# Fused patch embedding, attention and mixture-of-experts layer: the gate bias moves into the router's product, and its logits are read from PSUM

## The chip, the core and the metric

One core of a Trainium2 chip runs the whole program. The metric is the device time of one execution in microseconds (us); lower is better. Engines are named as in the profile: PE is TensorE (PEld its weight loads), DVE is VectorE, ACT is ScalarE, POOL is GpSimd, SP is the queue that issues DMAs.

## The reference

```
h   = patches(x) @ W.T + b + pos_emb                  # 64 images, 121 patches of 192
h   = concat([h, txt])                                # 249 tokens per image
h   = h + quantised_attention(layernorm(h))           # 12 heads, integer softmax
x2  = layernorm(h)
s   = softmax(x2 @ gate_w + gate_b)                   # the router: 16 experts
s_b = s + bias
    # best 4 of 8 pairs of experts by s_b, then the best 4 experts in them
w   = s of the chosen experts * 2.5                   # else 0
y   = sum_e w_e * (silu(x2 @ Wu_e + bu_e) * (x2 @ Wg_e + bg_e)) @ Wd_e + w @ bd + shared expert
out = h + y
```

What matters here is the line of `s`: a product of 192 by 16 per token, plus a bias of 16, and a softmax over the 16 values, for which their maximum is subtracted first.

## The kernel before

The kernel works image by image, 64 in all, as a software pipeline over five images at once. A list `ORDER` (L304 to L355) names every stage with a shift and a number, for instance `("turn", -1, 0)`: in step j this is stage "turn", number 0, of image j-1. Every engine walks through the same list and issues those stages that it has code for, in that order. There are no other priorities: each engine's queue is strictly in the list's order, and semaphores join the engines. Setup (weights rounded, scaled by LIFT = 256, transposed) comes first; on VectorE it is a chain in which each instruction waits for the one before (`link`, L685), and the other engines wait for the chain's count `VSETUP`.

The tokens of an image lie in two blocks of up to 128 partitions. The normalised rows x2 are kept as float16 (the rounded value twice, then the rounding rest) with three columns of ones behind them. They are transposed through PSUM to `x2T`, five blocks of 128 rows. The router's product ("route", L1155 to L1161) is ten matmuls of 16 columns, five blocks for each token block, against the weights `GW`; the fifth block's weights are the last 64 rows of the weight in rows 0 to 63 and zeros in rows 64 to 127, where rows 64 to 66 meet the ones. The expert products use the same three rows of ones for their biases, from `UGB`.

The PSUM bank `pX` (2 KB per partition) is shared by many products: patch embedding, the turns (transposes) of both normalised inputs, q/k, v, the transposed probabilities, the projection, the router, the chosen weights. PE keeps its order by `take_x(signal, value)` (L1056): before it writes pX it waits for the signal that its last user handed in, which tells that this content was read; and it hands in its own. The PSUM banks `pS` (scores and the exponent's polynomial), `pU` (expert products), `pW`, `pY`, `pO` have other users.

Around the router, `ORDER` (L334 to L336) has in this sequence, with the engine in brackets:

- route, image j-3 (PE), writes pX
- split, image j-1 (POOL): float16 parts of the first normalised input, read by turn
- act, pair 2 of image j-4 (DVE, L1028)
- logit, image j-3 (DVE, L1003): logits = pX / LIFT + bias, to SBUF
- lmax, image j-3 (DVE, L1008): maximum over the 16 values, of the SBUF logits
- expo, unit 2 of image j-2 (DVE, L962): four instructions, each with an accumulator read
- u, unit 3 of image j-2 (PE, L1120 and L1121): four matmuls to pS
- turn, number 0 of image j-1 (PE, L1082): three transposes to pX
- power, unit 3 of image j-2 (DVE, L953)
- mmG, pair 3 of image j-4 (PE, L1183): ten matmuls to pU
- below, unit 4 of image j-2 (ACT, L607)
- copy, number 0 of image j-1 (ACT, L650): reads the turn from pX
- below_max, image j-3 (DVE, L1012): difference of logits and maximum, to `lx`
- then square, unit 3 (ACT), quot, unit 4 (DVE, L948), gate, pair 3 of image j-4 (DVE, L1023, which needs mmG of pair 3), turn, number 1 (PE)

The gates stage (ACT, L662 and L663) then takes two Silu of the difference, from which the softmax's exponentials are made. The v product (PE, L1102 and L1104) is read from pX on DVE by L937. The shared down bias (L1192) is a product with the transposed chosen weights, which ACT copies (L668).

Of the kernel before, what the change touches and what calls it, by code (L numbers as in the profile page):

```python
# [14 lines left out]
ALU = mybir.AluOpType  # L15
# [6 lines left out]
F16 = mybir.dt.float16  # L22
# [20 lines left out]
def fused_layer(nc, x, txt, tok_W, tok_b, pos_emb, w_qkv, b_qkv, w_proj, b_proj, sw_qkv, sw_proj,  # L43
# [34 lines left out]
    with ctx:  # L78
        def sb(name, shape, dt=F32):
            return ctx.enter_context(nc.sbuf_tensor(name, shape, dt))  # L80
# [48 lines left out]
        def cut(words):  # L129
# [57 lines left out]
        pr8 = sb("pr8", [P, 2, D], I8)  # L187
        x2 = sb("x2", [P, 2, D])
        x2s = sb("x2s", [P, 2, BLOCKS * P], F16)
        logit = sb("logit", [P, 2, E])  # L190
        lmax = sb("lmax", [P, 2])
        lx = sb("lx", [P, 2, E])
        sil = sb("sil", [P, 2, 2, E])
# [25 lines left out]
        pY = ps("pY", [P, 512])  # L219
        pXb, pXh, pXi = (pX[:, :].bitcast(t) for t in (BF16, F16, I16))  # L220
        pXt = pX[:, :].rearrange("p (t c) -> p t c", t=2)[:, :, 0:D]
        pYt = pY[:, :].rearrange("p (t c) -> p t c", t=2)[:, :, 0:D]


# [19 lines left out]
            sem(n) for n in ("vr_done", "lo_done", "gr_done", "pr_done", "prT_ps"))  # L244
        prT_done, pv_done, o_q, ob_done, pj_ps, pq_done = (
            sem(n) for n in ("prT_done", "pv_done", "o_q", "ob_done", "pj_ps", "pq_done"))
        h2_done, g_ps, lg_done, rt_done, lx_done, sil_done = (
            sem(n) for n in ("h2_done", "g_ps", "lg_done", "rt_done", "lx_done", "sil_done"))
        w3_done, w3_ps, w3T_done, up_ps, gp_ps, wb_ps = (
            sem(n) for n in ("w3_done", "w3_ps", "w3T_done", "up_ps", "gp_ps", "wb_ps"))  # L250
        up_done, gate_done, act_done, dn_done, y_done = (
# [6 lines left out]
        def cc(n, rows=P):  # L258
            return cst[0:rows, n:n + 1]

        V_TOK, V_QKV, VSETUP = 4, 85, 102
        RT = 22


# [25 lines left out]
        for t in range(2):  # L290
# [41 lines left out]
            ("store", -5, -1), ("act", -4, 1), ("turn2", -3, 1), ("quot", -2, 3), ("copy2", -3, 1),  # L332
            ("pick", -4, 2), ("down", -4, 1), ("gate", -4, 2), ("silu", -4, 3), ("low", -2, 0),
            ("norm", -1, -1), ("low", -2, 1), ("top", -2, 5), ("route", -3, -1), ("split", -1, -1),  # L334
            ("act", -4, 2), ("logit", -3, -1), ("lmax", -3, -1), ("expo", -2, 2), ("u", -2, 3), ("turn", -1, 0),
            ("power", -2, 3), ("mmG", -4, 3), ("below", -2, 4), ("copy", -1, 0), ("below_max", -3, -1),  # L336
            ("peak", -2, 5), ("square", -2, 3), ("sum", -2, 2), ("quot", -2, 4), ("gate", -4, 3),
            ("turn", -1, 1), ("alpha", -2, 2), ("grow", -2, 0), ("expo", -2, 3), ("copy", -1, 1),
# [208 lines left out]
        def _(act):  # L547
# [43 lines left out]
            for j in STEPS:  # L591
                for stage, i, k in stages(j):
# [17 lines left out]
                    elif stage == "square":  # L610
                        n, b = NTOK[k % 2], k % 2
                        act.wait_ge(u_ps, UNITS * i + k + 1)
                        after(act, y_made, UNITS * i + k - 1)
                        sc_.activation(sq[b][0:n, :].rearrange("p (b c) -> p b c", b=2),  # L614
                                       pS[0:n, :, 0:2 * TOKENS], ACT.Square,
                                       bias=cc(C_HL, n)).then_inc(sq_done, 1)
                    elif stage == "share":
                        n, b = NTOK[k % 2], k % 2
                        act.wait_ge(al_done, UNITS * i + k + 1)
                        after(act, gr_done, UNITS * i + k - 1)  # L620
                        for m in range(PER):
                            c = slice(m * TOKENS, (m + 1) * TOKENS)
                            a = sc_.activation(v[b][0:n, c], y[b][0:n, c], ACT.Copy,  # L623
                                               scale=alpha[b][0:n, m:m + 1])
                        a.then_inc(vr_done, 1)
                    elif stage == "copyp":
                        n, b = NTOK[k % 2], k % 2
                        act.wait_ge(prT_ps, UNITS * i + k + 1)
                        after(act, pv_done, UNITS * i + k - 1)
                        pt = pXi.rearrange("p (m b q) -> p m b q", m=PER, b=2)  # L630
                        for t in range(2):
                            sc_.activation(probT[b][0:NTOK[t], :, t, 0:n].bitcast(I16),  # L632
                                           pt[0:NTOK[t], :, t, 0:n], ACT.Relu,
                                           bias=cc(C_OB, NTOK[t])).then_inc(prT_done, 1)
                    elif stage == "outq":
                        act.wait_ge(pv_done, UNITS * i + 2 * k + 2)
                        after(act, ob_done, GROUPS * (i - 1) + k + 1)
                        sc_.activation(o8[:, k, :], pO[:, 0:TOKENS], ACT.Copy,
                                       scale=cc(C_O)).then_inc(o_q, 1)
                    elif stage == "qkq":  # L640
                        act.wait_ge(qk_ps, QK * i + k + 1)
                        after(act, cv_done, GROUPS * (i - 1) + k % GROUPS + 1)
                        sc_.activation(qk8[:, k, :], pX[:, 0:TOKENS], ACT.Identity,  # L643
                                       bias=qk_bias[:, k:k + 1],
                                       scale=qk_scale[:, k:k + 1]).then_inc(qk_q, 1)
                    elif stage == "copy":
                        act.wait_ge(xt_ps[0], 2 * i + k + 1)
                        after(act, v_ps, i)
                        after(act, qk_ps, QK * i)
                        sc_.activation(xT[:, :, k * P:(k + 1) * P],  # L650
                                       pXh[:, 0:3 * P].rearrange("p (b c) -> p b c", b=3),
                                       ACT.Copy).then_inc(xt_done[0], 1)
                    elif stage == "copy2":
                        act.wait_ge(xt_ps[1], 2 * i + k + 1)
                        after(act, gp_ps, PAIRS * (i - 1))
                        after(act, g_ps, i - 1)
                        sc_.activation(x2T[i % 2][:, :, k * P:(k + 1) * P],
                                       pXh[:, 0:BLOCKS * P].rearrange("p (b c) -> p b c", b=BLOCKS),
                                       ACT.Copy).then_inc(xt_done[1], 1)
                    elif stage == "gates":  # L660
                        act.wait_ge(lx_done, i + 1)
                        sc_.activation(sil[:, 0], lx[:], ACT.Silu, bias=cc(C_DOWN)).then_inc(sil_done, 1)  # L662
                        sc_.activation(sil[:, 1], lx[:], ACT.Silu, bias=cc(C_UP),  # L663
                                       scale=-1.0).then_inc(sil_done, 1)
                    elif stage == "copyw":
                        act.wait_ge(w3_ps, i + 1)
                        after(act, wb_ps, (PAIRS - 1) * i)
                        sc_.activation(w3T[:], pXb[0:SPLIT * QUAD, 0:COLS], ACT.Copy).then_inc(w3T_done, 1)  # L668
                    elif stage == "silu":
                        n = EVEN if k == 0 else 2 * EVEN  # L670
                        act.wait_ge(up_ps, PAIRS * i + k + 1)
                        if k == 2:
                            act.wait_ge(dn_done, PAIRS * i + 1)
                        else:
                            after(act, gate_done, PAIRS * i + {0: 0, 1: -1}.get(k, k - 1))
                        sc_.activation(up[k % 2][:, 0:n], pU[:, 0, 0:n], ACT.Silu,  # L676
                                       scale=1.0 / LIFT).then_inc(up_done, 1)
# [3 lines left out]
        def _(dve):  # L681
# [125 lines left out]
            for b, p0, signal, n in ((1, REST, ld_f1, 10), (2, 0, ld_f2, 5)):  # L807
# [5 lines left out]
                for dst, src in ((UG[p0:P, b], ug_rows[b][p0:P]), (GW[p0:P, b, :], gw_rows[p0:P, b, :])):  # L813
                    if len(dst.shape) == 4:
                        dst, src = (a.rearrange("p e m h -> p (e m h)") for a in (dst, src))
                    link(stt(out=dst, in0=src, scalar=LIFT, in1=dst, op0=ALU.mult, op1=ALU.subtract))
            assert chain[0] == VSETUP, chain[0]

            dve.wait_ge(s_asetup, PSETUP)
# [84 lines left out]
            for j in STEPS:  # L904
                for stage, i, k in stages(j):
# [89 lines left out]
                    elif stage == "residual":  # L995
# [1 line left out]
                        after(dve, y_done, i - 1)  # L997
                        stt(out=h2[i % 2][:], in0=pr8[:], scalar=cc(C_S3), in1=h[i % 2][:], op0=ALU.mult,
                            op1=ALU.add).then_inc(h2_done, 1)
                    elif stage == "logit":  # L1000
                        dve.wait_ge(g_ps, i + 1)
                        after(dve, lx_done, i)
                        stt(out=logit[:].rearrange("p t e -> p (t e)"), in0=pX[:, 0:2 * E],  # L1003
                            scalar=1.0 / LIFT, in1=gb2[:].rearrange("p t e -> p (t e)"),
                            op0=ALU.mult, op1=ALU.add).then_inc(lg_done, 1)
                    elif stage == "lmax":
                        dve.wait_ge(lg_done, i + 1)
                        ve.tensor_reduce(lmax[:], logit[:], AX, ALU.max).then_inc(rt_done, 1)  # L1008
                    elif stage == "below_max":
                        dve.wait_ge(rt_done, RT * i + 1)  # L1010
                        after(dve, sil_done, 2 * i)
                        tt(lx[:], logit[:], lmax[:].unsqueeze(2).broadcast_to([P, 2, E]),  # L1012
                           ALU.subtract).then_inc(lx_done, 1)
                    elif stage == "gate":
                        m = EVEN if k == 0 else 2 * EVEN
# [22 lines left out]
        def _(pe):  # L1038
# [29 lines left out]
            for j in STEPS:  # L1068
                for stage, i, k in stages(j):
# [84 lines left out]
                        a.then_inc(pj_ps, 1)  # L1154
                    elif stage == "route":  # L1155
                        pe.wait_ge(xt_done[1], 2 * (i + 1))
                        take_x(lg_done, i + 1)
                        for t in range(2):
                            for m in range(BLOCKS):
                                a = mm(pX[:, t * E:(t + 1) * E], x2T[i % 2][:, m, t * P:(t + 1) * P],  # L1160
# [83 lines left out]
```

## Time and profile before

| | us |
|---|---|
| median of 3 runs (3519.58 to 3520.66) | 3520.66 |
| the profiled execution's own time | 3518.62 |
| its span, first to last instruction | 3516.8 |

| engine | busy us | share |
|---|---|---|
| PE | 3381.6 | 96% |
| DVE | 3368.5 | 96% |
| ACT | 3153.6 | 90% |
| POOL | 806.2 | 23% |

The profile is one execution; its time is 2.04 us below the median of the runs shown. Busy time is the union of an engine's instructions. Matmuls overlap each other in the array, so a matmul's duration (270 ns for 250 columns) is longer than the distance to the next one's start; pace is read from the starts.

### The profile page before, as it was taken

Reading aid. Unit: us, or ns where it says so; the run is one execution under the profiler, and the core shown is the slowest. Engines: PE = TensorE matmul, PEld = TensorE weight load, DVE = VectorE, ACT = ScalarE, POOL = GpSimd, SP = SyncE. Lnnn points to the kernel's source line nnn. Section 1 sums busy time; section 2 is a strip of 40 time slices with the busy share of each in tenths; the row PEclk is TensorE's granted clock in tenths of the full one; section 3 lists DMA queues with packets and bytes.
Section 4 is the critical chain, followed back from the end, with each engine's and each line's share of the span. In section 5 each row is a group of like instructions: output and inputs, shape, how many; then the busy total and the mean of one; then the engine's idle time right before and its main releaser. Section 6 shows DMA issues by size and latency. Waiting matters only on the chain.

```text
span 3516.8 us, 98077 instructions
## 1 busy us (share of the span) xinstructions
PE 3381.6 (96%) x30764; PEld 2898.6 (82%) x30764; DVE 3368.5 (96%) x10279; ACT 3153.6 (90%) x6228; POOL 806.2 (23%) x1647
## 2 busy tenths in 40 slices
PE   1589999999999999999999999999999999999999
PEld 1368888888888888888888888888888888888888
DVE  6699999999999999999999999999999999999995
ACT  2799999999999999999999999999999999999992
POOL 3222222222222222222221221222222222222210
PEclk9789999999999999999999999999999999999999
DMA  5101001000000000000000110100000000000000
GB/s 125 27 14 25 25 16 26 25 20 23 25 20 23 24 22 21 24 23 20 25 24 18 25 25 16 26 25 17 25 25 20 23 25 21 22 24 23 20 10 8
DMA packets 157123, 85.77 MB, mean 24 GB/s; under 512 B 51451, under 2 KB 154370, under 8 KB 156610
## 3 DMA queue, kind: packets, MB, share of 16 engines
q1 hardware_dynamic: 153692, 78.82, 9.0%
q8 instruction: 253, 4.15, 0.5%
q14 instruction: 260, 2.13, 0.2%
q10 hardware_dynamic: 2918, 0.67, 0.1%
HBM read 54.89 MB, written 12.24 MB: 19 GB/s over the span
## 4 chain that ended last, share of the span: by engine, by line
PE 92%; DVE 1%; issue 1%; ACT 0%; POOLq 0%; DVEq 0%; POOL 0%
PE pU L1183 33%; PE pY L1209 20%; PE pX L1075 5%; PE pX L1132 5%; PE pS L1120 4%; PE pS L1111 4%; PE pS L1121 4%; PE pX L1094 3%; PE pW L1195 3%; PE pO L1142 2%; PE pY L1192 1%; PE pX L1102 1%; PE pX L1088 1%; PE pX L1151 1%; PE pX L1082 1%
## 5 line engine op out<-in xcount | busy, mean ns | idle before, releaser
L1183 PE MATMUL pU<-x2T,UG 128*128 128x250 f16 x8704 | 1231.6, 270 | 1.0 <-ACT work L676 0.9
L1183 PEld LDWEIGHTS pU<-x2T,UG 128*128 128x128 f16 x8704 | 823.0, 97 | 108.7 <-ACT work L676 1.5
L1209 PE MATMUL pY<-WD,work 128*128 128x192 f32 (+1 forms) x4352 | 810.0, 328 | 0.0
L1209 PEld LDWEIGHTS pY<-WD,work 128*128 128x128 f32 (+1 forms) x4352 | 690.8, 187 | 3.9
L962 DVE SCALAR_TENSOR_TENSOR work<-work,cst 128x249 f32<-128x249 f32 (+1 forms) x1536 | 658.6, 484 | 8.4 <-issue 4.3
L623 ACT ACTIVATE work<-work,alpha 128x249 f32<-128x249 f32 (+1 forms) x1536 | 648.3, 509 | 15.2 <-DVE alpha L974 14.0
L607 ACT ACTIVATE work<-a,room 128x249 bf16<-128x249 int8 (+1 forms) x1536 | 648.3, 514 | 0.0
L1183 PE MATMUL pU<-x2T,UGB 67*128 67x250 f16 x2176 | 592.4, 272 | 0.0
L942 DVE TENSOR_REDUCE rmax<-a 128x4 f32<-128x996 int8 (+1 forms) x384 | 452.9, 1179 | 40.9 <-ACT a L598 40.9
L632 ACT ACTIVATE passing<-pX,cst 128x512 int16<-128x512 int16 (+3 forms) x768 | 480.8, 687 | 6.9 <-PE pX L1132 3.5
L598 ACT ACTIVATE a<-pS,cst 128x996 int8<-128x996 f32 (+1 forms) x384 | 421.4, 1097 | 70.3 <-PE pS L1111 70.1
L614 ACT ACTIVATE work<-pS,cst 128x996 f32<-128x996 f32 (+1 forms) x384 | 419.5, 1092 | 56.8 <-PE pS L1121 56.8
L983 DVE SCALAR_TENSOR_TENSOR work<-work 128x996 bf16<-128x996 bf16 (+1 forms) x384 | 453.1, 1180 | 0.1
L497 POOL TENSOR_SCALAR qb<-qk 128x249 bf16<-128x249 int8 x192 | 103.6, 540 | 1308.6 <-ACT qk L643 1307.5
L676 ACT ACTIVATE work<-pU 128x500 f32<-128x500 f32 (+1 forms) x576 | 326.0, 566 | 72.6 <-PE pU L1183 72.6
L1023 DVE TENSOR_TENSOR work<-pU,work 128x500 f32<-128x500 f32 x512 | 342.0, 668 | 17.3 <-PE pU L1183 17.1
L1028 DVE TENSOR_TENSOR work<-work,pW 128x500 f32<-128x500 f32 x512 | 339.2, 662 | 13.3 <-PE pW L1195 12.6
L1120 PE MATMUL pS<-work,ident 128*128 128x498 bf16 (+1 forms) x768 | 293.3, 382 | 7.7 <-ACT a L598 2.8
L1121 PE MATMUL pS<-work,identx 128*128 128x498 bf16 (+1 forms) x768 | 290.5, 378 | 0.0
L1111 PE MATMUL pS<-kb,qz 128*128 128x249 bf16 (+1 forms) x1536 | 232.6, 275 | 29.1 <-DMA qz<-qb 21.0
L979 DVE TENSOR_SCALAR work<-work 128x996 int16<-128x996 int16 (+1 forms) x384 | 255.2, 665 | 0.8 <-ACT work L623 0.7
L643 ACT ACTIVATE qk<-pX,qk_bias,qk_scale 128x249 int8<-128x249 f32 x384 | 219.1, 570 | 39.6 <-PE pX L1094 39.5
(209 smaller groups left out, 5337.5 us busy)
## 6 DMA issues: line engine op xcount, KB each, us to landing
img<-in_x_dram SPq DMA_DIRECT2D x896, 23.5 KB
img<-in_x_dram SPq DMA_DIRECT2D x768, 21.4 KB
qz<-qb SPq DMA_DIRECT2D x768, 15.6 KB, 1.8
h<-in_txt_dram SPq DMA_DIRECT2D x64, 96.0 KB, 2.0
out_dram<-yout SPq DMA_DIRECT2D x64, 96.0 KB
out_dram<-yout SPq DMA_DIRECT2D x64, 90.8 KB
WD<-in_L_ffn_Wd_dram SPq DMA_DIRECT2D x1, 1536.0 KB, 7.6
work<-in_L_ffn_Wu_dram SPq DMA_DIRECT2D x2, 512.0 KB, 6.6
```

Of the source, the lines that this page charges most:

```text
L598: sc_.activation(a8[b][0:n, :].rearrange("p (b c) -> p b c", b=2), pS[0:n, :, 0:2 * TOKENS], ACT.Copy, scale=cc(C_S, n)).then_inc(a_done, 1)
L607: a = sc_.activation(g16[b][0:n, c], a8[b][0:n, c], ACT.Relu, bias=room[b][0:n, m:m + 1])
L614: sc_.activation(sq[b][0:n, :].rearrange("p (b c) -> p b c", b=2), pS[0:n, :, 0:2 * TOKENS], ACT.Square, bias=cc(C_HL, n)).then_inc(sq_don ...
L623: a = sc_.activation(v[b][0:n, c], y[b][0:n, c], ACT.Copy, scale=alpha[b][0:n, m:m + 1])
L632: sc_.activation(probT[b][0:NTOK[t], :, t, 0:n].bitcast(I16), pt[0:NTOK[t], :, t, 0:n], ACT.Relu, bias=cc(C_OB, NTOK[t])).then_inc(prT_don ...
L942: ve.tensor_reduce(rmax[b][0:n, :], a8[b][0:n, :].rearrange("p (m c) -> p m c", m=PER), AX, ALU.max).then_inc(mx_done, 1)
L962: a = stt(out=y[b][0:n, c], in0=sq[b][0:n, c], scalar=cc(C_KC, n), in1=pw[b][0:n, c].bitcast(BF16), op0=ALU.add, op1=ALU.mult, accum_out=r ...
L983: stt(out=grown[b][0:n, :], in0=p16[b][0:n, :].bitcast(BF16), scalar=6.0, in1=v[b][0:n, :], op0=ALU.subtract, op1=ALU.mult).then_inc(gr_do ...
L1120: mm(pS[0:n, m, 0:2 * TOKENS], ident[0:n, 0:n], g16[b][0:n, c], start=True, stop=False)
L1121: a = mm(pS[0:n, m, 0:2 * TOKENS], identx[0:n, 0:n], q16[b][0:n, c], start=False, stop=True)
L1183: a = mm(pU[:, s, q * EVEN:(q + 1) * EVEN], weights, x2T[i % 2][0:w, m, 0:EVEN], start=m == 0, stop=m == BLOCKS - 1)
L1209: a = mm(pY[0:n, t * 256:t * 256 + D], (act_[k % 2] if k else up[0])[:, c:c + n], WD[:, e, :], start=k == 0 and t == 0, stop=e == E - 1, s ...
```

## The change

The bias is put into the router's product: it is scaled by LIFT, split into three float16 parts, and the parts are written into rows 64, 65 and 66 of the fifth weight block, where the ones are. The product in PSUM is then LIFT times the complete logits. The logit stage is dropped from `ORDER`; maximum and difference read the lifted values from PSUM, and the gates divide by LIFT in their scale. The bank pX after the router is handed on by the signal of the difference (`lx_done`) in place of that of the logit (`lg_done`). `gb2` is still loaded. Nothing else in `ORDER` moves.

```diff
-        logit = sb("logit", [P, 2, E])
+        gb_parts = sb("gb_parts", [P, SPLIT, E], F16)
...
+        lifted = pX[:, 0:2 * E].rearrange("p (t e) -> p t e", t=2)
...
-        V_TOK, V_QKV, VSETUP = 4, 85, 102
+        V_TOK, V_QKV, VSETUP = 4, 85, 111
...
-            ("act", -4, 2), ("logit", -3, -1), ("lmax", -3, -1), ("expo", -2, 2), ("u", -2, 3), ("turn", -1, 0),
+            ("act", -4, 2), ("lmax", -3, -1), ("expo", -2, 2), ("u", -2, 3), ("turn", -1, 0),
...
-                        sc_.activation(sil[:, 0], lx[:], ACT.Silu, bias=cc(C_DOWN)).then_inc(sil_done, 1)
+                        sc_.activation(sil[:, 0], lx[:], ACT.Silu, bias=cc(C_DOWN),
+                                       scale=1.0 / LIFT).then_inc(sil_done, 1)
                         sc_.activation(sil[:, 1], lx[:], ACT.Silu, bias=cc(C_UP),
-                                       scale=-1.0).then_inc(sil_done, 1)
+                                       scale=-1.0 / LIFT).then_inc(sil_done, 1)
...
+            ones3 = slice(REST, ONES)
+            whole = gb2[ones3, 0, :]
+            link(ts(whole, whole, LIFT, None, ALU.mult))
+            for s in range(SPLIT):
+                if s:
+                    link(tt(whole, whole, gb_parts[ones3, s - 1], ALU.subtract))
+                link(ve.tensor_copy(gb_parts[ones3, s], whole))
+            link(ts(GW[ones3, 3, :], gb_parts[ones3, 0], identf[ones3, REST:REST + 1], None, ALU.mult))
+            for s in range(1, SPLIT):
+                link(stt(out=GW[ones3, 3, :], in0=gb_parts[ones3, s], scalar=identf[ones3, REST + s:REST + s + 1],
+                         in1=GW[ones3, 3, :], op0=ALU.mult, op1=ALU.add))
...
-                    elif stage == "logit":
+                    elif stage == "lmax":
                         dve.wait_ge(g_ps, i + 1)
                         after(dve, lx_done, i)
-                        stt(out=logit[:].rearrange("p t e -> p (t e)"), in0=pX[:, 0:2 * E],
-                            scalar=1.0 / LIFT, in1=gb2[:].rearrange("p t e -> p (t e)"),
-                            op0=ALU.mult, op1=ALU.add).then_inc(lg_done, 1)
-                    elif stage == "lmax":
-                        dve.wait_ge(lg_done, i + 1)
-                        ve.tensor_reduce(lmax[:], logit[:], AX, ALU.max).then_inc(rt_done, 1)
+                        ve.tensor_reduce(lmax[:], lifted, AX, ALU.max).then_inc(rt_done, 1)
                     elif stage == "below_max":
                         dve.wait_ge(rt_done, RT * i + 1)
                         after(dve, sil_done, 2 * i)
-                        tt(lx[:], logit[:], lmax[:].unsqueeze(2).broadcast_to([P, 2, E]),
+                        tt(lx[:], lifted, lmax[:].unsqueeze(2).broadcast_to([P, 2, E]),
                            ALU.subtract).then_inc(lx_done, 1)
...
                     elif stage == "route":
                         pe.wait_ge(xt_done[1], 2 * (i + 1))
-                        take_x(lg_done, i + 1)
+                        take_x(lx_done, i + 1)
```

## Rows read from the trace of the kernel before

**Rows 1.** The page, busy time by engine: us, share of the span, instructions.
```profile
PE 3381.6 (96%) x30764; PEld 2898.6 (82%) x30764; DVE 3368.5 (96%) x10279; ACT 3153.6 (90%) x6228; POOL 806.2 (23%) x1647
PE 92%; DVE 1%; issue 1%; ACT 0%; POOLq 0%; DVEq 0%; POOL 0%
```

**Rows 2.** Busy table by stretch, steady part; then granted clock, DMA share and GB/s.
```profile
600.00:1600.00 1000.00, 998.55 (x9192) 862.52 (x9190) 989.02 (x3047) 934.79 (x1858) 232.70 (x479) 1.00 0.09 22
...
2006.40:2058.60 52.20, 52.16 (x483) 45.11 (x481) 51.65 (x160) 48.90 (x98) 12.17 (x25) 1.00 0.09 23
```

**Rows 3.** Timeline of PE around one router (start, us, operation); last, weight loads of turn.
```profile
2003.63 0.40 PE L1160 MATMUL pX<-GW,x2T 128*128 128x16 f16 x10
...
2004.76 0.33 PE L1082 MATMUL pX<-ident,xs 128*128 128x128 f16 x3
2004.93 0.59 PE L1183 MATMUL pU<-x2T,UG 128*128 128x250 f16 x4
...
2005.46 0.59 PE L1183 MATMUL pU<-x2T,UG 128*128 128x250 f16 x4
2005.89 0.27 PE L1183 MATMUL pU<-x2T,UGB 67*128 67x250 f16 x1
...
L1082 PEld LDWEIGHTS pX<-ident,xs 128*128 128x128 f16 x384 | 32.2, 99 | 25.9 <-POOL xs L534 9.5 <-issue 4.6
```

**Rows 4.** Timeline of DVE over the same stretch.
```profile
2004.31 0.18 DVE L1003 SCALAR_TENSOR_TENSOR logit<-pX,gb 128x32 f32<-128x32 f32 x1
2004.53 0.19 DVE L1008 TENSOR_REDUCE lmax<-logit 128x2 f32<-128x32 f32 x1
2004.71 0.48 DVE L962 SCALAR_TENSOR_TENSOR work<-work,cst 128x249 f32<-128x249 f32 x1
...
2006.32 0.41 DVE L953 TENSOR_SCALAR work<-work 121x996 int16<-121x996 int16 x1
2006.65 0.18 DVE L1012 TENSOR_TENSOR lx<-logit,lmax 128x32 f32<-128x32 f32 x1
...
2007.27 0.67 DVE L1023 TENSOR_TENSOR work<-pU,work 128x500 f32<-128x500 f32 x1
```

**Rows 5.** Instructions on the logit tile: ns least/median/most, first and last start.
```profile
L1003 DVE SCALAR_TENSOR_TENSOR logit<-pX,gb x64: 173/179/192, 174.4 to 3458.3; 128x32 f32<-128x32 f32 x64
...
L1012 DVE TENSOR_TENSOR lx<-logit,lmax x64: 181/183/191, 176.7 to 3458.8; 128x32 f32<-128x32 f32 x64
```

**Rows 6.** Waits of 600 to 3000 us; then the timeline at one v product.
```profile
DVE v L937 <- PE pX L1104: 13.9, 44, 0.4
...
1829.70 0.25 PE L1104 MATMUL pX<-v_add,ones 128*128 128x192 bf16 x1
...
1829.99 0.56 DVE L937 TENSOR_TENSOR v<-pX,v_scale 128x384 int8<-128x384 f32 x1 [0.32 <-PE pX L1104]
```

**Rows 7.** Timeline of the start-up.
```profile
52.47 32.54 SPq L378 DMA_DIRECT2D UGB<-b_parts  x51
...
62.24 0.17 DVE L816 SCALAR_TENSOR_TENSOR GW<-gw_rows,GW 128x16 f16<-128x16 f32 x1
62.46 0.35 DVE L910 TENSOR_TENSOR h<-pX,pos 121x192 f32<-121x192 f32 x1
...
98.21 1.02 PE L1111 MATMUL pS<-kb,qz 128*128 128x249 bf16 x4 [21.04 <-DMA qz<-qb]
```

**Rows 8.** Timeline of PE at one shared down bias.
```profile
1788.44 0.66 PE L1192 MATMUL pY<-BD,w3T 96*128 96x192 bf16 x6 [0.30 <-ACT w3T L668]
```

**Rows 9.** Start-up: timeline of PE, then the busy table with the granted clock.
```profile
110.93 0.39 PE L1120 MATMUL pS<-work,ident 121*121 121x498 bf16 x1 [1.27 <-ACT work L614]
...
166.09 0.61 PE L1111 MATMUL pS<-kb,qz 128*121 128x249 bf16 x4 [1.27 <-ACT a L598]
...
167.10:170.50 3.40, 1.38 (x4) 0.59 (x5) 3.32 (x8) 3.40 (x8) 3.00 (x6) 0.50 0.25 58
...
132.90:136.30 3.40, 2.76 (x12) 1.85 (x13) 3.23 (x11) 2.43 (x7) 1.94 (x3) 0.51 0.02 5
```

More of the change, by code:

```diff
@@ L246, in fused_layer @@
             sem(n) for n in ("prT_done", "pv_done", "o_q", "ob_done", "pj_ps", "pq_done"))
-        h2_done, g_ps, lg_done, rt_done, lx_done, sil_done = (
-            sem(n) for n in ("h2_done", "g_ps", "lg_done", "rt_done", "lx_done", "sil_done"))
+        h2_done, g_ps, rt_done, lx_done, sil_done = (
+            sem(n) for n in ("h2_done", "g_ps", "rt_done", "lx_done", "sil_done"))
         w3_done, w3_ps, w3T_done, up_ps, gp_ps, wb_ps = (
```

## The prediction

> **What bounds the kernel now.** I read the page's engine line first: TensorE is busy 96% of the span and VectorE 96% [rows 1], so neither the matmuls nor the vector work can be dismissed. The busy table by stretch then takes the start-up out of the average: in a thousand microseconds of the steady part PE is busy 998.55 and VectorE 989.02, and in one image's period of 52.20 us PE is busy 52.16 and VectorE 51.65 [rows 2]. The reader is to see that PE has 0.04 us of visible idle per image and VectorE 0.55. The chain of waits puts nearly everything on PE, and the timeline agrees: five matmuls of 250 columns start within 0.53 us (2004.93 to 2005.46, [rows 3]), about 0.106 us each, with no step between stages. PE is the bound, VectorE is just behind it. The wait table of the steady part has only one regular wait of VectorE for PE, at the v product: 13.9 us in 44 images, 0.3 us each [rows 6]. A saved VectorE instruction therefore buys nothing by itself; a wait put into PE's queue costs its full length.
>
> **The operation removed.** The logit instruction takes 179 ns, 64 times [rows 5], and the next dependent one starts 0.22 us after it [rows 4]. That is 0.22 us per image, 14 us in all, taken from VectorE, which is not the bound. Its gain is only that maximum, four exponent instructions, power and difference come 0.22 us earlier.
>
> **Maximum and difference read PSUM.** No row shows these two on PSUM. The nearest is the logit instruction itself: reading 32 elements from PSUM took 179 ns, the difference of 32 elements from SBUF 183 ns [rows 5]. So I take 0, with 0 and +0.05 us per image as ends. The Trainium skill (VectorE: DVE Perf Modes, the section on the TRN2 errata) gives VectorE instructions with a PSUM source a fixed 120 cycles against 58 at 0.96 GHz: an estimate of 0.065 us more for each of the two, which speaks against this change. By that rule the sum would be 61 x 0.13 = 8 us longer; the 179 against 183 ns does not bear it out.
>
> **Bias in the product, scale in the gates.** The router still issues ten matmuls; the three rows of the last weight block were zero and are streamed already. The two gate activations get another immediate scale. Both cost nothing, without needing cover.
>
> **Setup.** Nine small chained VectorE instructions are added (three casts, two subtractions, one scaling, three combinations). The nearest takes 0.17 us and the following one starts 0.22 us after it [rows 7], so 9 x 0.2 = 1.8 us, before the first normalisation. It is covered: the SP queue issues the late bias rows from 52.47 us for 32.54 us, and PE stands idle 21.04 us until 98.21 for the first query DMA, issued behind them [rows 7]. I cost it at nothing; without that cover, 1.8 us once.
>
> **The order of the shared PSUM bank.** This is the step that decides. PE may overwrite pX after the router's product only when its reader is done. The reader was the logit instruction; now it is the difference. Between router and next user (the first turn of image i+2) PE has only the u product: router at 2003.63, turn at 2004.76 [rows 3]. Before, logit ran from 2004.31 to 2004.49, so turn found the bank free [rows 3, 4]. In VectorE's order, between maximum and difference, stand four exponent instructions (2004.71 to 2006.32, a pitch of 0.40 us) and power (0.33 us to the next start): the difference starts at 2006.65 [rows 4]. Nothing in the change moves it forward except the 0.22 us of logit. So:
> - the difference starts at 2006.65 - 0.22 = 2006.43 and ends at 2006.61;
> - an inter-engine hand-over took 0.04 us at the v product (the last matmul ends at 1829.95, v starts at 1829.99) [rows 6], and the turn's weight load takes 0.10 us [rows 3]: turn's matmul at 2006.75;
> - it ran at 2004.76, so PE stands 1.99, say 2.00 us per image, of which some 1.8 are visible as idle.
>
> Behind the waiting turn in PE's queue stand mmG of pair 3, the second turn, mmU of pair 4 and the q/k products. ScalarE's copy waits for the turn, and square behind it. VectorE waits at the gate of pair 3: its matmuls visibly end at 2006.16 [rows 3] and would end 2.00 later, 2008.16, while VectorE would be there at 2007.27 - 0.22 = 2007.05 [rows 4]. So VectorE, too, loses 1.1 us at once.
>
> **Can the delay be made up within the image?** VectorE runs 1.1 - 0.22 = 0.9 us late against PE's 2.0, but where it already waits for PE, at v, it takes on PE's whole lateness [rows 6]. From there to the next router both carry the same 2.0, and the next difference comes 2.0 late again. PE's one larger gap, 0.30 us at the shared down bias, waits for ScalarE's copy [rows 8], behind work that VectorE releases, so it stays. I recover nothing; the bound is that 0.30 us, and 0.24 us if VectorE reached maximum right when the product lands (2003.63 + 0.40 + 0.04 = 2004.07 instead of 2004.31 [rows 3, 4]). That leaves 1.46 us as the low end per image, 2.1 as the high one.
>
> **Sum.** 62 images have a router product followed by a turn; the first lies in the start-up, where PE idles anyway. 61 x 2.00 = 122 us. The profiled execution took 3518.62 us (span 3516.8), so 3640.6. The median of the runs shown is 3520.66, 2.04 above it: **3643 us**.
>
> **Rivals.**
> *Shorter stall.* Part of PE's lateness is recovered as above, or VectorE leads. 1.46 to 1.9 us in 61 images is 89 to 116 us: 3610 to 3637; a little more hidden slack would make it 3600. For it: latencies hide small gaps in PE's row. Against: PE's pitch never relaxes. Chance 0.20.
> *The stall also lowers the clock.* The granted clock is 1.0 throughout the steady part [rows 2], where PE never stands for long. In the start-up PE stood 1.27 us before 110.93 and the next matmul still took 0.39 us; it stood 1.27 us before 166.09 too, and the stretch from 167.10 shows 0.50 [rows 9], the lower level, 1.2 GHz. A new idle of 1.8 us in each image lies above both. The shortest slow stretch there, 132.90 to 136.30 at 0.51 [rows 9], did 3.4 us x 0.5 = 1.7 us less work. If a third of the images pay it, 20 x 1.7 = 34 us more: 3677; if all, 3747. Against: around the new gap PE works densely, in the start-up it doesn't. Chance 0.22.
> *Faster: VectorE is the true bound.* If PE's busy row hid 2.0 us of slack per image between turn and v, PE would catch up before v, and the 0.22 us x 64 = 14 us of the logit stage would show: 3507. It decides from 2.0 us of hidden slack on. Against: the 0.106 us pitch and the 0.04 us of idle; and the 1.1 us new wait at the gate of pair 3 falls on VectorE itself. Chance 0.03.
> *The new wait does not bind*, because turn waits for something as late anyway: no change, 3520. Against: turn started at full pitch after u [rows 3]. Chance 0.02.
> The remaining 0.03 is for a stall that grows beyond 2.1 us per image, by ScalarE falling behind too: 3650 and above.
>
> **How the numbers follow.** The forecast has 0.50. The range 3608 to 3702 takes in it, most of the shorter stall and the clock case up to 35 falls (3643 + 59); about 0.2 is left outside. 0.2% of the time, 7 us, is about what a measurement of this kernel can tell from no change. Faster by more 0.03, within 0.02, slower by more 0.95.
>
> **What would show it.** Right: a PE idle of some 1.8 us before turn (L1082's place) released by the difference, in some 61 images; a new VectorE wait of about 1.1 us at the gate multiplication; the period from difference to difference 54.2 instead of 52.2 us; maximum and difference at 180 to 190 ns; the first score matmul still near 98 us. Wrong: a period of 52 us; a turn released by anything else; maximum or difference near 250 ns; a granted clock below 1.0 in the steady part (the clock rival); a gate that doesn't wait (then VectorE leads).

## The result and the profile after

The changed kernel takes 3660.22 us (median of 3, 3658.25 to 3662.45) against 3520.66 before: ratio 1.0399, 95% interval 1.0384 to 1.0413. That is 139.6 us more, where 122 were forecast, inside the range.

The page first, engine line and chain, to be held against [rows 1]:

```profile
PE 3414.9 (93%) x30764; PEld 2908.9 (80%) x30764; DVE 3380.3 (92%) x10224; ACT 3162.7 (86%) x6228; POOL 778.6 (21%) x1647
PE 3%; DVE 1%; issue 0%; ACT 0%; POOLq 0%; POOL 0%; DVEq 0%
```

TensorE has fallen from 96% to 93% and VectorE from 96% to 92%. The chain, 92% on PE before, now accounts for 4% of the span: it can't be followed through, so it names nothing. The wait table of the whole run does (who waited, for whom: total, times, longest):

```profile
PE pX L1090 <- DVE lx L1020: 108.1, 62, 2.0
```

L1090 is the turn, L1020 the difference: 62 waits, one per image with a router followed by a turn, 1.74 us each. There was no such row before. The timeline of PE around one router, answering to [rows 3], and of VectorE, to [rows 4]:

```profile
2139.48 0.40 PE L1168 MATMUL pX<-GW,x2T 128*128 128x16 f16 x10
2140.39 0.37 PE L1129 MATMUL pS<-work,identx 121*121 121x498 bf16 x1
2142.51 0.33 PE L1090 MATMUL pX<-ident,xs 128*128 128x128 f16 x3 [1.74 <-DVE lx L1020]
2143.64 0.27 PE L1191 MATMUL pU<-x2T,UGB 67*128 67x250 f16 x1
```

```profile
2140.15 0.18 DVE L1016 TENSOR_REDUCE lmax<-pX 128x2 f32<-128x32 f32 x1
2140.25 0.47 DVE L975 SCALAR_TENSOR_TENSOR work<-work,cst 128x249 f32<-128x249 f32 x1
...
2141.85 0.42 DVE L966 TENSOR_SCALAR work<-work 121x996 int16<-121x996 int16 x1
2142.18 0.19 DVE L1020 TENSOR_TENSOR lx<-pX,lmax 128x32 f32<-128x32 f32 x1
...
2144.01 0.68 DVE L1031 TENSOR_TENSOR work<-pU,work 128x500 f32<-128x500 f32 x1 [1.13 <-issue]
```

The last of the u matmuls starts at 2140.39 and would be followed at a pitch of 0.21, at 2140.60; the turn starts at 2142.51. The stall is 1.91 us. The turn starts 0.14 us after the difference ends (2142.18 + 0.19). VectorE pays in its turn: 1.13 us idle at the gate of pair 3. The row names no releaser ("issue"), but the pair's matmuls end visibly at 2143.64 + 0.27 = 2143.91, and the gate starts at 2144.01.

The bank read by maximum and difference costs nothing, as against [rows 5] (ns least/median/most, first and last start):

```profile
L1016 DVE TENSOR_REDUCE lmax<-pX x64: 175/182/192, 176.3 to 3600.0; 128x2 f32<-128x32 f32 x64
L1020 DVE TENSOR_TENSOR lx<-pX,lmax x64: 174/182/191, 178.4 to 3600.2; 128x32 f32<-128x32 f32 x64
```

and the maximum before, from SBUF:

```profile
L1008 DVE TENSOR_REDUCE lmax<-logit x64: 185/186/189, 174.6 to 3458.6; 128x2 f32<-128x32 f32 x64
```

The difference took 183 ns from SBUF and takes 182 from PSUM; the maximum took 186 and takes 182.

There is a second loss. The busy table from one difference to the next, three images in a row, then two stretches of the middle one, answering to [rows 2] and [rows 9] (the third number from the end is the granted clock):

```profile
1978.38:2032.40 54.02, 52.25 (x480) 44.98 (x480) 51.76 (x160) 48.94 (x97) 11.69 (x25) 1.00 0.09 22
2032.40:2088.15 55.75, 53.95 (x480) 45.95 (x480) 51.85 (x159) 49.17 (x97) 11.60 (x25) 0.97 0.08 21
2088.15:2142.18 54.03, 52.25 (x480) 44.97 (x480) 51.78 (x160) 48.94 (x97) 11.69 (x25) 1.00 0.09 22
...
2033.00:2037.00 4.00, 4.00 (x27) 3.15 (x26) 1.71 (x4) 2.83 (x6) 0.00 (x0) 0.61 0.02 4
2037.00:2041.00 4.00, 4.00 (x35) 3.28 (x33) 4.00 (x13) 3.73 (x11) 0.00 (x0) 1.00 0.00 0
```

A period without a fall of the clock is mostly 54.03 to 54.13 us (52.12 to 52.22 before); in either kernel a few are 0.2 to 0.5 us longer. In the middle one the clock is at the lower of its two levels, 1.2 GHz, for most of the stretch right behind the gap: 27 matmuls in 4 us where the next 4 us hold 35, and the period is 1.65 us longer. Counted from the starts of all 64 differences, 14 of the 58 periods of the steady part are long in this way, 44 are not. The trace has just 14 stretches of low clock there, and each begins within 0.5 us behind a turn that had waited. The kernel before has none. Such counts are those of one profiled execution of each kernel; the times of the others, 1 to 7 us apart, leave room for a few falls more or less. So the 139.6 us are 61 x 1.92 = 117 for the wait, plus 14 x 1.65 = 23 for the clock, 140 in all.

### The profile page after: what moved, and what is told of

Its sections match the earlier page's. It is cut to its first block and busy times, and to the rows that moved or that the text cites. A ratio compares the mean times of both kernels' runs of the same rounds, so it can differ in the third digit from the quotient of the medians.

```text
span 3658.4 us, 98022 instructions
## 1 busy us (share of the span) xinstructions
PE 3414.9 (93%) x30764; PEld 2908.9 (80%) x30764; DVE 3380.3 (92%) x10224; ACT 3162.7 (86%) x6228; POOL 778.6 (21%) x1647
## 5 line engine op out<-in xcount | busy, mean ns | idle before, releaser
L1191 PE MATMUL pU<-x2T,UG 128*128 128x250 f16 x8704 | 1251.5, 272 | 1.1 <-ACT work L678 0.9
L1191 PEld LDWEIGHTS pU<-x2T,UG 128*128 128x128 f16 x8704 | 832.0, 98 | 115.6 <-ACT work L678 1.5
L498 POOL TENSOR_SCALAR qb<-qk 128x249 bf16<-128x249 int8 x192 | 78.5, 409 | 1473.0 <-ACT qk L644 1473.0
```

The lines of the kernel that those rows point to most:

```text
L1191: a = mm(pU[:, s, q * EVEN:(q + 1) * EVEN], weights, x2T[i % 2][0:w, m, 0:EVEN], start=m == 0, stop=m == BLOCKS - 1)
```

## The experiments

Ratios are to the kernel before, run on the same chip. The theory: the time is lost because the bank pX is handed on by the difference, and the loss is the way of VectorE to the difference less what PE has to do meanwhile. The rivals: reading PSUM, the bias rows or the setup cost it; VectorE is the bound; the idle itself, by way of the clock, is the larger part.

### The difference moved ahead of the exponents

```diff
-  ("act", -4, 2), ("lmax", -3, -1), ("expo", -2, 2), ("u", -2, 3), ("turn", -1, 0),
+  ("act", -4, 2), ("lmax", -3, -1), ("below_max", -3, -1), ("expo", -2, 2), ("u", -2, 3), ("turn", -1, 0),
-  ("copy", -1, 0), ("below_max", -3, -1),
+  ("copy", -1, 0),
```

> The changed kernel with one stage moved: the difference directly behind the maximum, ahead of the four exponent instructions and power. Hand-over theory: the difference ends 0.4 us after the maximum starts, and the u product on PE covers that, so the stall of turn goes altogether: 3520 us within 5, PE idle before turn below 0.1 us per image, granted clock 1.0 in the steady part. Rival 1 (the cost lies in reading PSUM, in the bias rows or in the setup): nothing of it depends on the order, 3650 to 3660. Rival 2 (VectorE is the true bound, and the missing logit shows once the wait is gone): 3507 to 3512.

3527.15 us, ratio 1.0019 (1.0010 to 1.0028). All but 7 of the 139.6 us come back with one entry of a list moved, everything else of the change in place: rival 1 falls. The hand-over theory expected 3520 within 5 and no stall left, so it missed by 2 us. The 7 are some 0.11 us in each period (mostly 52.24 to 52.33). Their place, in the timelines of VectorE and PE:

```profile
2009.93 0.19 DVE L1020 TENSOR_TENSOR lx<-pX,lmax 128x32 f32<-128x32 f32 x1
...
2009.94 0.37 PE L1129 MATMUL pS<-work,identx 121*121 121x498 bf16 x1
2010.26 0.33 PE L1090 MATMUL pX<-ident,xs 128*128 128x128 f16 x3
```

PE would be free at 2009.94 + 0.21 = 2010.15, the difference ends at 2010.12, the turn starts 0.14 later, at 2010.26. No row calls this an idle: the last u matmul, lasting 0.37, covers it. The same wait is left at 0.11 us.

### The rest of the wait covered

```diff
-  ("expo", -2, 2), ("u", -2, 3), ("turn", -1, 0),
+  ("expo", -2, 2), ("u", -2, 3), ("pick", -4, 3), ("turn", -1, 0),
-  ("pick", -4, 3), ("below", -2, 5), ("silu", -4, 4),
+  ("below", -2, 5), ("silu", -4, 4),
```

> As the first experiment (difference directly behind the maximum), and the product that spreads the weights of pair 3 (two matmuls, 0.21 us on PE) moved from behind mmG of pair 4 to just ahead of turn. Theory: the 0.11 us per image by which that kernel was slower than the one before is the rest of the same hand-over (difference ends at 2010.12, turn starts at 2010.26, PE free at 2010.15); 0.21 us of work in between covers it: 3520 within 3, ratio 1.000, period 52.17. Rival (the 0.11 us are a cost of reading PSUM or of VectorE's order): stays at 3527.

3520.67 us against 3519.33, ratio 1.0004 (0.9995 to 1.0013); periods mostly 52.12 to 52.23 again. The theory holds to 0.1 us per image. It is also the verdict on the idea itself: with no wait left, dropping 64 VectorE instructions gains nothing that can be measured. Rival 2 of the first experiment (3507) falls with it. VectorE waits the saved time away at v: 0.4 us per image in the stretch from 600 to 3000 us, where [rows 6] have 0.3.

```profile
DVE v L950 <- PE pX L1112: 19.2, 46, 0.5
```

### The wait shortened, lengthened, and put in alone

Difference between exponents and power:

```diff
-  ("turn", -1, 0), ("power", -2, 3),
+  ("turn", -1, 0), ("below_max", -3, -1), ("power", -2, 3),
...
-  ("copy", -1, 0), ("below_max", -3, -1),
+  ("copy", -1, 0),
```

> The changed kernel with the difference between the exponent instructions and power, so 0.33 us earlier than in the change and 1.6 us later than directly behind the maximum. Hand-over theory: the stall follows the place of the difference one to one: 1.90 - 0.33 = 1.57 us per image, 61 x 1.57 = 96 us, 3616 without falls of the clock; with a third to all of the falls of the changed kernel (15 x 1.65 us) 3616 to 3640. Rival (a fixed cost of any late hand-over): same as the change, 3660.

Difference behind the next quotient:

```diff
-  ("below_max", -3, -1), ("peak", -2, 5), ("square", -2, 3), ("sum", -2, 2), ("quot", -2, 4),
+  ("peak", -2, 5), ("square", -2, 3), ("sum", -2, 2), ("quot", -2, 4), ("below_max", -3, -1),
```

> The changed kernel with the difference 0.5 us later still, behind the next quotient (and the sum). Hand-over theory: stall 1.90 + 0.52 = 2.42 us per image, 61 x 2.42 = 148 us, 3668 without falls of the clock. Clock theory: an idle of 2.2 us visible per image lowers the clock more often than one of 1.75 us (15 images in the change): 20 to 40 images x 1.65 us, 3700 to 3735. If the falls depend on where the gap lies against a fixed beat rather than on its length, their number may also drop to none: 3668.

And the kernel before with a single line changed:

```diff
-                        take_x(lg_done, i + 1)
+                        take_x(lx_done, i + 1)
```

> The kernel before with one line of the change: the router hands its bank on by the signal of the difference; the logit stage, the bias addition and the SBUF reads stay. Hand-over theory: the whole loss and a little more, since logit stands ahead of the maximum again: the difference at 2006.65 instead of 0.32 earlier, a stall of 2.2 us per image, 61 x 2.2 = 134 us, 3655 without falls of the clock, up to 3690 with them. Rival 1 (PSUM reads or bias rows cost the time): 3520 to 3530.

| kernel | us | ratio (95% interval) | mean of the periods without a fall | long periods |
|---|---|---|---|---|
| before | 3520.66 | | 52.22 | 0 |
| before power | 3617.35 | 1.0277 (1.0263 to 1.0291) | 53.81 | 0 |
| the change | 3660.22 | 1.0399 (1.0384 to 1.0413) | 54.13 | 14 |
| hand-over alone | 3669.24 | 1.0426 (1.0411 to 1.0440) | 54.44 | 10 |
| behind quot | 3677.80 | 1.0446 (1.0432 to 1.0460) | 54.66 | 5 |

The period grows by 1.59, 1.92, 2.22 and 2.44 us (from unrounded means). The prediction had 2.00 for the change; from its measured 1.90 the expectations took 1.57, 2.2 and 2.42 for the other three. The wait goes one to one with the place of the difference, and the one line in the kernel before gives the whole loss, with logit, SBUF reads and bias addition still there. Its row in the wait table of the stretch from 600 to 3000:

```profile
PE pX L1082 <- DVE lx L1012: 91.9, 44, 2.4
```

The clock theory put on record for the kernel with the longest gap, 20 to 40 falls and 3700 to 3735 us, was wrong: longer gaps did not bring more falls than the change's 14 but fewer. In the steady part of the hand-over kernel one of the ten stretches of low clock lasted twice as long, and its period was 57.33 us.

### What the falls of the clock depend on

```diff
-                        for q in range(2):
+                        for q in (0, 1, 0, 1, 0, 1) if k == 8 else (0, 1):
                             a = mm(pW[:, q * EVEN:(q + 1) * EVEN], pick[:, 2 * k - 2 + q, :], w3T[:, 0:EVEN],
```

> The changed kernel, and for pair 8 the two matmuls that spread the weights are issued three times over (same operands, same place in PSUM): 0.43 us more work on PE per image, half a period away from the gap, which stays as it is (1.74 us visible). Theory that the falls of the clock follow the gap alone: 14 falls again, 3660 + 61 x 0.43 = 3686. Theory that their number depends on how the image's period falls against a fixed rhythm of the chip: another number (the fourth experiment, period 54.6, had 5 in the steady part), 0 to 6 falls, 3520 + 61 x 2.34 = 3663 up to 3673.

3666.75 us, ratio 1.0419 (1.0403 to 1.0434), and 2 long periods in the steady part in place of 14. The gap is untouched, as its row shows (600 to 3000 us):

```profile
PE pX L1090 <- DVE lx L1020: 77.3, 44, 2.0
```

The changed kernel has this row in the same stretch, to the digit. So the gap makes a fall possible but doesn't decide it; another 0.43 us of work half an image away takes 12 of 14 away. Whether the work does it or the period that it lengthens to 54.56 us, this run does not separate.

Next the gap is filled with repeats of one product, or holds that product once (the same diff without its change of the loop over `q`):

```diff
-  ("expo", -2, 2), ("u", -2, 3), ("turn", -1, 0),
+  ("expo", -2, 2), ("u", -2, 3), ("pick", -4, 3), ("turn", -1, 0),
...
-  ("pick", -4, 3), ("below", -2, 5), ("silu", -4, 4),
+  ("below", -2, 5), ("silu", -4, 4),
...
-                        for q in range(2):
+                        for q in (0, 1) * 8 if k == 3 else (0, 1):
                             a = mm(pW[:, q * EVEN:(q + 1) * EVEN], pick[:, 2 * k - 2 + q, :], w3T[:, 0:EVEN],
```

> The changed kernel with the gap on PE filled: the product that spreads the weights of pair 3 moved ahead of turn and issued eight times (1.7 us of matmuls whose results are all the same), so PE works while VectorE is on its way to the difference. Hand-over theory: turn starts when the difference is done, whatever PE does meanwhile: the 1.90 us stay, less the 0.21 us of this product that no longer stand elsewhere: 3520 + 61 x 1.69 = 3623. Clock theory: no idle, no falls, clock 1.0 in the steady part. Rival (repeated matmuls delay turn, or PE's work rather than VectorE sets the time): above 3635.

> As g2, with the product issued once: the gap is 0.21 us shorter than in the change (1.5 us visible), the rest idle. Without falls 3623, the same as g2; with as many falls as the change 3646. The second experiment had none at 1.4 us visible. The difference to g2 is what the idle, rather than the wait, costs.

Filled: 3626.58 us, ratio 1.0306 (1.0289 to 1.0323), no long period. Issued once: 3625.09 us, ratio 1.0300 (1.0285 to 1.0316), one long period. The timeline of PE in the filled one, and the turn in the other:

```profile
2547.30 1.87 PE L1203 MATMUL pW<-w3T,pick 96*128 96x250 bf16 x16
2549.21 0.33 PE L1090 MATMUL pX<-ident,xs 128*128 128x128 f16 x3
```

```profile
2550.84 0.33 PE L1090 MATMUL pX<-ident,xs 128*128 128x128 f16 x3 [1.53 <-DVE lx L1020]
```

PE visibly busy throughout or idle for 1.53 us: the time is the same within 2 us, and both were expected at 3623. In the filled kernel too the turn waits: it starts 0.3 us or more behind the last product's start in every image of the steady part, where 0.11 is full pace, and 0.15 us after the difference ends. This separates the two losses, and the idle is not the larger: in the change it is 23 of 140 us. The wait is paid whether or not a busy share shows it; the idle costs something of its own only where the clock falls. The filled kernel also looks, by its busy table from 600 to 3400 us, like one bound by PE:

```profile
600.00:3400.00 2800.00, 2793.85 (x25656) 2405.09 (x25654) 2690.92 (x8201) 2541.31 (x5038) 605.45 (x1298) 1.00 0.09 22
```

### Is VectorE really free?

```diff
+        spare = [sb(f"spare{n}", [P, 2, E]) for n in range(2)]
...
                         ve.tensor_reduce(lmax[:], logit[:], AX, ALU.max).then_inc(rt_done, 1)
+                        for n_ in range(2):
+                            tt(spare[n_][:], logit[:], gb2[:], ALU.add)
```

> The kernel before with two more small VectorE additions behind the maximum (0.1 us each, results unused), about as much as the logit stage takes. PE-bound theory: VectorE has the 0.3 us per image that it waits at v, so nothing: 3520 within 3. VectorE-bound rival: 64 x 0.2 = 13 us more, 3533.

3526.23 us, ratio 1.0020 (1.0011 to 1.0029): 7 us. The PE-bound theory expected nothing, the rival 13 us, from 0.2 us per image. What the additions really add to VectorE's queue is in its timeline:

```profile
2008.02 0.19 DVE L1009 TENSOR_REDUCE lmax<-logit 128x2 f32<-128x32 f32 x1
2008.12 0.28 DVE L1011 TENSOR_TENSOR spare<-logit,gb 128x32 f32<-128x32 f32 x2
2008.32 0.47 DVE L963 SCALAR_TENSOR_TENSOR work<-work,cst 128x249 f32<-128x249 f32 x1
```

From the maximum to the exponents it is 0.30 us, where [rows 4] have 0.18 (0.19 in most images). The additions lengthen the queue by 0.11 us, and 64 x 0.11 = 7 us. So the rival's price was too high, and priced rightly it comes true: the added work is paid in full. For added work this run is against the theory that VectorE is free; only for saved work does the covered version show it.

VectorE's wait at v shrinks from 0.3 us to 0.2 but doesn't vanish (wait table, 600 to 3000 us), so v is not where it binds:

```profile
DVE v L938 <- PE pX L1107: 6.5, 39, 0.2
```

The timelines show another place, just behind a turn of the probabilities. In the kernel with more vector work:

```profile
2026.46 0.67 DVE L1031 TENSOR_TENSOR work<-work,pW 128x500 f32<-128x500 f32 x1
...
2026.59 0.62 PE L1135 MATMUL pX<-ident,passing 128*128 128x128 bf16 x8
2027.18 0.39 PE L1198 MATMUL pW<-w3T,pick 96*128 96x250 bf16 x2
```

and before:

```profile
1813.25 0.68 DVE L1028 TENSOR_TENSOR work<-work,pW 128x500 f32<-128x500 f32 x1
...
1813.68 0.62 PE L1132 MATMUL pX<-ident,passing 128*128 128x128 bf16 x8
1814.13 0.38 PE L1195 MATMUL pW<-w3T,pick 96*128 96x250 bf16 x2
```

The product of pair 6 (pick) waits until pW was read for pair 5. Before, the reader ended at 1813.93 and pick ran when its turn came, 0.45 us behind the first of the transposes. Now the reader ends at 2027.13 and pick starts 0.05 later, 0.59 behind them: 0.14 us more. This is regular: of 48 images of the steady part the wait is there in all 48 with the additions, in 6 before. In the other 42 the reader had ended 0.21 us or more ahead of the product, mostly 0.24, where 0.06 is enough, so VectorE had some 0.18 us of room at this one place. Why 0.11 us of additions uses up all of it has not been followed. A saved instruction gains nothing, an added one does cost.

### An attempt to beat both

The largest gap that the trace before shows on PE is at the shared down bias [rows 8], 0.57 us between matmul starts. It is not the usual case: in 43 of 46 images from 600 to 3000 us the distance there is 0.28 to 0.33 us and shows no idle, where 0.11 would be full pace. Two kernels move ScalarE's copy ahead of the four share instructions, one on top of the covered version, one on the kernel before:

```diff
-  ("norm2", -3, -1), ("share", -2, 0), ("score", -2, 5), ("chosen", -4, -1),
-  ("top", -2, 4), ("copyw", -4, -1), ("mmU", -4, 2),
+  ("norm2", -3, -1), ("copyw", -4, -1), ("share", -2, 0), ("score", -2, 5), ("chosen", -4, -1),
+  ("top", -2, 4), ("mmU", -4, 2),
```

> As f1, and ScalarE's copy of the chosen weights moved ahead of the four share instructions in front of it. Theory that PE's last gap (0.46 us between matmul starts at the shared down bias, 0.30 of it shown as idle) is now the largest thing left: copy is ready about 0.8 us earlier, the gap closes, and VectorE, relieved of the logit, can follow: 52.17 - 0.3 to 0.46 us per image, 3492 to 3502. Rival (share and the quantisation behind it come late, and the gap opens elsewhere): 3520 or slower.

> The kernel before (with its logit stage) and the same move of ScalarE's copy alone. If VectorE is just behind PE, it becomes the bound here and part of the gain is lost: its 51.65 busy plus 0.25 us of dependent starts are 51.9 per image, 3505. So f2 should be up to 14 us faster than this one if the logit's 0.22 us is worth something once PE's gap is gone; if both are equal, the logit stage costs nothing in either.

3556.56 us (ratio 1.0107, 1.0093 to 1.0121) and 3555.51 (1.0102, 1.0087 to 1.0118). The gap does close: the distance is 0.11 us in all images of both. But where a gain was expected (3492 to 3502, and 3505), both lose: the period grows by 0.6 us. The rival was right that gaps open elsewhere. The copy now stands ahead of the four share instructions, and PE waits for ScalarE in other places, in the first of the two kernels (600 to 3000 us):

```profile
PE pX L1096 <- ACT x2T L658: 12.6, 45, 0.3
PE pS L1128 <- ACT a L599: 7.0, 39, 0.2
```

Two further waits, 0.3 and 0.2 us, are most of the 0.6; the rest shows no idle. Both kernels lose the same, with and without logit, so the logit stage costs nothing here either. No version here beats the kernel before.

## Why the prediction was right, point by point

- **What bounds.** A wait put into PE's queue cost its full length: 2 us per image could not be made up anywhere, and the period grew by the wait itself in all kernels that had one. A saved VectorE instruction bought nothing, as foretold. That VectorE's slack is at v was only half the truth: it has 0.3 us there, but some 0.18 at pair 6's pick, and 0.11 us of added work was paid in full.
- **Logit removed.** Costed as 0.22 us earlier. Measured, maximum to difference is 2.03 us where logit to difference was 2.34, so 0.31 earlier: 0.22 for the stage itself, and the exponents now start 0.10 us behind the maximum (2140.15, 2140.25) and not 0.18 as in [rows 4]. This term was mis-sized by 0.09 us and brought the wait from 2.00 to 1.91, some 5 us less in all.
- **PSUM reads.** Costed at 0, measured 182 against 183 ns, and 182 against 186. The estimate of 0.065 us more for each of the two, from the cycle table in the Trainium skill (VectorE: DVE Perf Modes, the section on the TRN2 errata), is not borne out for these 32 elements.
- **Bias rows, gate scale, setup.** Costed at 0. The version with the wait covered contains all three and is at 1.0004. The first score matmul starts at 98.13 us, 98.21 before, so the SP queue did cover the longer setup.
- **Hand-over.** 0.04 and 0.10 us for the weight load; measured 0.14.
- **VectorE's new wait.** 1.1 us at the gate of pair 3 foretold, 1.13 measured. The rest of the path was wrong. The prediction let VectorE take over PE's remaining lateness at v, so the wait there should have grown from 0.3 us to some 1.4. It grew to 0.5, and the first experiment, whose PE is hardly late at all, has 24.1 us in 46 images at v, also 0.5 each. So the growth belongs to the missing logit, not to PE's lateness. The wait table from 600 to 3000 us shows where VectorE stood instead (gate, v, exponents):

```profile
DVE work L1031 <- issue: 62.3, 49, 2.3
DVE v L950 <- PE pX L1112: 23.5, 44, 0.6
DVE work L975 <- issue: 18.2, 58, 0.8
```

  Counted from the maximum (medians of 48 images), the gate comes 1.1 us later than before (3.85 us against 2.74), the next row maximum (`rmax`) 1.9 (23.63, 21.73) and v 2.1 (37.00, 34.88). Most of the lateness had been taken on ahead of v, much of it at the exponents. The sum did not suffer: what it needed was that nothing is recovered, and nothing was.
- **Recovery.** The low end of 1.46 us leaned on the 0.30 us of [rows 8], which only 3 of 46 images have. None of it was recovered.
- **Rivals.** The forecast and the clock rival turned out to hold together; a granted clock below 1.0 in the steady part stood in the prediction's list of signs of being wrong, and it came. The rival supposed a third of the images and 1.7 us each; 14 images at 1.65 us are 23 us. This is the term missing from the sum: 3643 - 5 + 23 = 3661. Its price per fall was right, its 20 falls were a guess, and it was kept as an alternative when it was an addition. Nothing in the prediction gives 14 falls and no run here explains the number, so that the total came out only 17 us above the forecast is in part luck.
- **Slower, faster.** The shorter stall, the bound on VectorE and the wait that doesn't bind did not happen.

## What to carry to other kernels

Where a buffer is handed on by the signal of its last reader, a fusion that removes the copy makes that last reader later. Ask what stands between the old reader and the new one in that engine's queue, and subtract what the writer has to do meanwhile: that is the price per pass if the writer is the bound. Move the new reader forward in the same edit. And a removed instruction on an engine that is 96% busy may still be worth nothing, while an added one costs.

## What was not expected of the hardware

- The number of falls of TensorE's clock did not follow the length of the gap: 14 with 1.74 us of visible idle, 5 in the kernel with the longest gap, 2 with the same 1.74 us and 0.43 us more work elsewhere, 1 with 1.53 us, none in the one with the wait a third of a microsecond shorter. In the change they often came in every third image: the differences that open a long period stand at 557.38, 721.21, 885.15 and 1049.00 us, three periods apart each time. The image's period seems to take part, since the kernel behind quot has a longer gap and period, no more work, and fewer falls; what decides was not tried and stays open. Each fall cost 1.6 to 1.7 us, apart from the one of double length.
- The distance between the starts of small VectorE instructions is no fixed price. The difference starts 0.22 us behind the maximum that it reads (2009.71, 2009.93 in the first experiment). The exponents read neither of the two, yet start 0.19 us behind the maximum before, 0.18 behind the difference in the first experiment and 0.10 behind the maximum in the change; an addition starts 0.10 behind the maximum. Why they differ was not tried. Taking away the logit stage freed 0.31 us for this reason and not its own 0.22.
